# 64-column attention tiles, 64 queries of each image to a maxima tile, transposed reciprocals, and a GpSimd that waits for VectorE's sums

## What is computed

```python
Q = jnp.einsum('kc,bcp->bkp', q_w, xf)   # 16 x 3136
K = jnp.einsum('kc,bcp->bkp', k_w, xf)
V = jnp.einsum('vc,bcp->bvp', v_w, xf)   # 64 x 3136
S = jnp.einsum('bkp,bkq->bpq', Q, K)
A = jax.nn.softmax(S, axis=-1)
z = jnp.einsum('bpq,bvq->bvp', A, V)
```

## Time and profile before

| what | value |
|---|---|
| median of 3 runs | 2080.59 us (2080.13 to 2082.37) |
| the profiled execution's own time | 2084.49 us |
| its span, from first to last instruction | 2082.7 us |
| mean granted TensorE clock, of 2.4 GHz | 0.924 |
| busy share of the span: PE, DVE, ACT, POOL | 90%, 77%, 42%, 64% |

### The profile page before, as it was taken

One profiled execution on the slowest core, in us unless ns is written; L12 is line 12 of the kernel. 1 busy time (PEld: TensorE's weight loads), 2 busy tenths in 40 slices (PEclk: granted clock), 3 DMA queues, 4 the chain that ended last, 5 costly groups with the idle time before them and its releaser, 6 DMA issues.

```text
span 2082.7 us, 30055 instructions
## 1 busy us (share of the span) xinstructions
PE 1869.7 (90%) x7932; PEld 696.8 (33%) x7932; DVE 1596.4 (77%) x2642; ACT 865.8 (42%) x1064; POOL 1341.5 (64%) x702
## 2 busy tenths in 40 slices
PE   5877999999878799999987789999998779999996
PEld 4352222223336122222333622222233442222221
DVE  5747888887874788888786478888879557888883
ACT  2132554546314145454622324545461333454553
POOL 3510788989650179898954037989886205798887
PEclk9986999999888699999988869999999887999998
DMA  1003000000000300000000210000000030000000
GB/s 76 0 0 78 1 6 5 5 8 7 6 1 12 66 1 6 10 5 4 5 6 1 37 41 6 5 5 5 4 5 5 0 47 0 6 5 5 4 4 9
DMA packets 8505, 26.08 MB, mean 13 GB/s; under 512 B 2256, under 2 KB 5840, under 8 KB 7888
## 3 DMA queue, kind: packets, MB, share of 16 engines
q1 hardware_dynamic: 8400, 24.79, 5.1%
HBM read 8.73 MB, written 6.42 MB: 7 GB/s over the span
## 4 chain that ended last, share of the span: by engine, by line
PE 63%; issue 13%; DVE 10%; POOL 9%; ACT 2%; SPq 1%; DMA 1%; POOLq 1%; DVEq 0%; ACTq 0%
PE PS L1165 27%; PE PS L1112 14%; PE PS L1097 11%; DVE nmt L617 3%; DVE nmt L610 2%; POOL accP L943 2%; DVE accD L694 2%; POOL VT L905 1%; PE PS L1083 1%; POOL VT L900 1%; POOL VT L902 1%; PE PS L1070 1%; PE PS L1061 1%; POOL VT L909 1%; PE PS L1122 1%
## 5 line engine op out<-in xcount | busy, mean ns | idle before, releaser
L826 ACT ACTIVATE Pb<-PS 128x896 f32<-128x896 f32 (+1 forms) x700 | 640.5, 917 | 629.2 <-PE PS L1112 611.4
L943 POOL TENSOR_TENSOR accP<-accP,Pb 128x896 f32<-128x896 f32 x364 | 832.3, 2287 | 46.3 <-ACT Pb L826 20.5
L610 DVE TENSOR_REDUCE nmt<-PS 128x1 f32<-128x448 f32 x1176 | 663.6, 613 | 164.1 <-PE PS L1097 163.2
L1165 PE MATMUL PS<-Pb,VT 128*64 128x448 f32 x2800 | 693.5, 573 | 11.9 <-ACT Pb L826 9.3
L1112 PE MATMUL PS<-Qa,Ka 99*128 (+3 forms) x1400 | 478.3, 363 | 1.0 <-ACT Qa L810 1.0
L1097 PE MATMUL PS<-Ka,Qa 96*128 96x448 bf16 x1176 | 394.4, 356 | 24.3 <-DVE nmt L610 23.4
L694 DVE TENSOR_TENSOR accD<-accD,Pb 128x896 f32<-128x896 f32 x168 | 301.8, 1796 | 42.2 <-ACT Pb L826 40.6
L1112 PEld LDWEIGHTS PS<-Qa,Ka 99*128 99x128 bf16 (+1 forms) x1400 | 125.1, 98 | 540.5 <-issue 490.2
L936 POOL TENSOR_TENSOR accQ<-Pb 128x896 f32<-128x896 f32 x28 | 61.7, 2203 | 267.2 <-ACT Pb L826 267.2
L1165 PEld LDWEIGHTS PS<-Pb,VT 128*64 128x64 f32 x2800 | 145.7, 136 | 239.0 <-issue 193.5
L526 DVE SCALAR_TENSOR_TENSOR Pb<-PS,cf,xnp 128x448 f32<-128x448 f32 x252 | 154.8, 675 | 12.6 <-PE PS L1020 8.8
(11 more groups left out here) (138 smaller groups left out, 1488.4 us busy)
## 6 DMA issues: line engine op xcount, KB each, us to landing
xin<-in_x SPq DMA_DIRECT2D x4, 1568.0 KB, 6.6
out<-xw SPq DMA_DIRECT2D x28, 224.0 KB, 1.9
Qa<-parts SPq DMA_DIRECT2D x48, 98.0 KB, 4.0
Ka<-parts SPq DMA_DIRECT2D x48, 98.0 KB, 4.1
wz<-in_weights SPq DMA_DIRECT2D x1, 829.0 KB, 7.9
cs<-in_cst SPq DMA_DIRECT2D x1, 576.0 KB, 8.5
wz<-in_weights SPq DMA_DIRECT2D x1, 576.0 KB, 9.4
cs<-in_cst SPq DMA_DIRECT2D x1, 256.0 KB, 6.3
```

The costliest lines, as they stand in the source:

```text
L610: nc.vector.reduce_max(nmt[:, i // NJ, i % NJ:i % NJ + 1], PS[0:BLK, bank, 0:CH], X, negate=True).then_inc(mx_free, 1)
L826: nc.scalar.activation(Pb[0:r, j % PSLOTS, :, :], PS[0:r, b:b + 2, 0:CH], ACT.Exp).then_inc(exp_done, 1)
L943: nc.gpsimd.tensor_tensor((accQ if j < TO_ACCP else accP)[:, :, :], (accQ if j <= TO_ACCP else accP)[:, :, :], Pb[:, j % PSLOTS, :, :], AL ...
L1165: last = mm(PS[C * h:C * h + C, OB, 0:CH], VT[:, j, C * h:C * h + C], Pb[:, j % PSLOTS, h, :], start=(j == 0), stop=(j == NQ - 1))
```

## The change

- Maxima tiles: a tile is now 64 queries of each of the two images by 448 keys, made by two matmuls of 64 columns that write the lower and the upper 64 partitions of one bank (`tile_of`). A superblock has 7 x 7 = 49 tiles; 49 instead of 56 come before the first step. PSUM rows, maxima and split are laid out accordingly.
- Scores: 128 keys are made by two matmuls of 64 columns instead of one of 128.
- SP issues the spreading DMAs by part, both halves of a part together, and TensorE waits for both halves before the first tile.
- Reciprocals: one 32 x 32 block transpose of the denominators (each is equal over 64 partitions), a reciprocal of 14 columns, and a transpose back with the 14 columns broadcast, all three in step 3, instead of four reciprocals of 112 columns in steps 3 to 6.
- GpSimd waits for VectorE's sum of step j-1 before its own sum of step j (at steps 4, 8, 12, 16, 20), and at step 1 for all sums of the superblock before.
- The superblocks of a group are written out one by one on TensorE and VectorE.

```diff
-TILES = 2 * NJ
-PAIR_TILES = 7 * TILES
-FIRST_TILES = 4 * TILES
+TILES = NJ * NJ
+GROUP_TILES = (NJ - 1) * TILES
...
-                for h in range(2):
-                    for part, ready in enumerate((part_h, part_m, part_l)):
-                        if h == 0:
-                            sp.wait_ge(ready, NJ * g + NJ)
+                for part, ready in enumerate((part_h, part_m, part_l)):
+                    sp.wait_ge(ready, NJ * g + NJ)
+                    for h in range(2):
                         spread(part, h)
...
-                def reciprocals(sidx, i):
-
-                    if i == 0:
-                        dve.wait_ge(d_ready, sidx + 2)
-                        dve.wait_ge(fin_done, sidx + 1)
-                    ins = nc.vector.reciprocal(Rr[:, i * QUART:(i + 1) * QUART], PS[:, 7, i * QUART:(i + 1) * QUART])
-                    if i == 3:
-                        ins.then_inc(recip, 1)
+                def reciprocals(sidx):
+
+                    dve.wait_ge(d_ready, sidx + 2)
+                    dve.wait_ge(fin_done, sidx + 1)
+                    nc.vector.transpose(Rr[:, :], PS[:, 7, 0:CH]).then_inc(rstep, 1)
+                    dve.wait_ge(rstep, 2 * sidx + 1)
+                    nc.vector.reciprocal(Rc[:, :], Rr[:, 0:CH:SQ]).then_inc(rstep, 1)
+                    dve.wait_ge(rstep, 2 * sidx + 2)
+                    nc.vector.transpose(Rr[:, :].rearrange("p (a b) -> p a b", b=SQ),
+                                        Rc[:, :].unsqueeze(2).to_broadcast([P, CH // SQ, SQ])).then_inc(recip, 1)
...
                             pool.wait_ge(exp_done, NQ * sidx + j + 1)
                             if j == 1:
+                                pool.wait_ge(psum_dve, NDVE * (sidx + 1))
+                            if j - 1 in DVE_SUMS:
+                                pool.wait_ge(psum_dve, NDVE * (sidx + 1) + dve_sums_upto(j - 1))
+                            if j == 1:
...
+                def tile_of(bank, s, i):
+
+                    blk, t = i // NJ, i % NJ
+                    for h in range(2):
+                        last = mm(PS[C * h:C * h + C, bank, 0:CH], Qa[0:KROWS, h, s * CH + blk * C:s * CH + blk * C + C],
+                                  Ka[0:KROWS, h, t * CH:(t + 1) * CH], start=True, stop=True)
+                    return last
...
                     j = k % NQ
-                    r = key_rows(j)
-                    ins = mm(PS[0:r, 2 * (k % 2) + h, 0:CH], Ka[0:KROWS + 3, h, j * QC:j * QC + r],
-                             Qa[0:KROWS + 3, h, ds(s * CH, CH)], start=True, stop=True)
+                    for c in range(0, key_rows(j), C):
+                        ins = mm(PS[c:c + C, 2 * (k % 2) + h, 0:CH], Ka[0:KROWS + 3, h, j * QC + c:j * QC + c + C],
+                                 Qa[0:KROWS + 3, h, s * CH:(s + 1) * CH], start=True, stop=True)
...
-                for i in range(FIRST_TILES):
-                    h, blk, t = i // (FIRST_TILES // 2), i // NJ % 4, i % NJ
-                    if i % (FIRST_TILES // 2) == 0:
-                        pe.wait_ge(qk_loaded[h], 16 * (SPREADS * (g + 1) + 1))
+                for loaded in qk_loaded:
+                    pe.wait_ge(loaded, 16 * (SPREADS * (g + 1) + 1))
+                for i in range(TILES):
```

More of the change, by code:

```diff
@@ L43 @@
 KROWS = 6 * DK
-QUART = CH // 4
+SQ = 32
 BLK = 128
@@ L78, in plan_tiles @@
 def plan_tiles():
-    plan, steps, held = [], [], {4: 0, 5: 0, 7: 0}
-    early = 3 * TILES
-    for span, tiles in ((range(0, SPLIT_STEP + 1), early),
-                        (range(SPLIT_STEP + 1, NQ + SPLIT_STEP + 1), PAIR_TILES - early)):
-        total = sum(DENSITY[i % NQ] for i in span)
-        done = 0
-        for i in span:
-            steps += [i] * (round(tiles * (done + DENSITY[i % NQ]) / total) - round(tiles * done / total))
-            done += DENSITY[i % NQ]
-    for i, step in enumerate(steps):
-        banks = (4, 5, 7) if step % NQ in FREE7 else (4, 5)
-        bank = min(banks, key=lambda b: held[b])
-        plan.append((step, bank, held[bank]))
-        held[bank] = i + 1
+    plan, held = [], {4: 0, 5: 0, 7: 0}
+    for s in range(1, NJ):
+        end = NQ * (s - 1) + SPLIT_STEP + 1
+        span = range(0 if s == 1 else end - NQ, end)
+        total = sum(DENSITY[k % NQ] for k in span)
+        done = 0
+        for k in span:
+            upto = done + DENSITY[k % NQ]
+            for _ in range(round(TILES * upto / total) - round(TILES * done / total)):
+                bank = min((4, 5, 7) if k % NQ in FREE7 else (4, 5), key=lambda b: held[b])
+                plan.append((k, bank, held[bank]))
+                held[bank] = len(plan)
+            done = upto
     return plan
@@ L695, in superblock @@
                                                         ALU.add).then_inc(psum_dve, 1)
[L697 removed]
+                for i in range(TILES):
                     first_tile(i)
[L699 to L712 removed]
+                dve.wait_ge(first_used, TILES * (g + 1) + NJ)
+                split_max(NJ * g)
+                for s in range(NJ):
+                    superblock(s)
+                reciprocals(NJ * g + NJ - 1)
             front_stats(0)
@@ L827, in exps @@
                                              ACT.Exp).then_inc(exp_done, 1)
-                        if j == ROWS_STEP + 2 and rows_of:
-                            max_rows(sidx + 1, *rows_of)
+                        if j == ROWS_STEP + 2 and rows_of is not None:
+                            max_rows(sidx + 1, rows_of)
                         if front_of is not None:
@@ L1141, in front_at, with superblock @@
                             front_transpose(g + 1, i)
-                def superblock(s, half, base, col, first):
+                def superblock(s):
                     sidx = NJ * g + s
@@ L1149, in superblock @@
                     for j in range(NQ):
-                        k = NQ * (half % 2) + j
-                        tiles = [] if half == 2 else [i for i in tiles_at(k) if not first or i >= EARLY_TILES]
+                        k = NQ * s + j
+                        tiles = [i for i in tiles_at(k) if i >= EARLY_TILES]
                         def next_tile(seen7):
@@ L1203, in group @@
                         scores(j, 0, h)
-                pair_of(0, True)
-                with pe.Fori(1, NJ // 2) as t:
-                    pair_of(t, False)
-                superblock(NJ - 1, 2, 0, 0, False)
+                for s in range(NJ):
+                    superblock(s)
                 denominators(NJ * g + NJ - 1)
```

124 lines of the change are left out of this document (50 added, 74 removed).

## The result

The changed kernel takes 2124.4 us (median of 4 runs, 2120.6 to 2131.9) against 2081.5 for the kernel before beside it: 1.0208 of its time, 95% interval 1.0192 to 1.0224, 43 us slower. The forecast was 2101, 21 us slower: the sign was right, the size half. The profiled span is 2124.3 us, 41.6 more than before.

What follows compares the result with a forecast made beforehand. TensorE was taken to set the pace, GpSimd and VectorE close behind, its saving lost to GpSimd's longer round. Terms 4.8 + 2.2 + 1.9 - 4.0 + 0.4 = 5.3 us a group, 21 in four: 2101 us, range 2035 to 2125.

Steps and rivals of the forecast that it cites:

- TensorE's part: TensorE's work in a superblock: a step of 1.53 instead of 1.78 us, about 40.5 us in all, some 7 less.
- GpSimd's part, superblocks 1 to 4: Walk from denominators to denominators: 48.4 us a round, 193.6 for four against 191.4 before, +2.2 us a group.
- Theory A: Follow-up experiments' theory: a superblock's round is closed by GpSimd's wait for step 3's copy, 4.1 us behind the denominators.
- the wait of step 4: GpSimd's sum of step 4 waits for VectorE's copy, starting 4.05 us after the denominators; TensorE's saved 7 us become waiting.
- Superblock 0: First superblock of a group: no denominators before it, GpSimd's new wait short, -4.0 us a group off 57.2.
- Superblock 6: Last superblock of a group: +2.3 us for GpSimd's steps 4 and 20, -1.9 for shorter reciprocals, +0.4 a group.
- Superblock 5: Superblock without tiles in its last steps: 47.3 us instead of 45.4, +1.9 us a group.
- the held banks: At a superblock's end, reductions behind VectorE's late sum hold TensorE's two banks; worth 1.2 us a round.
- Before the first step: Start of a group: first tile 8.5 us later, waiting for all 24 DMAs; fewer reductions -3.7; +4.8 us a group.
- The faster one: Rival: GpSimd's waits find VectorE done, the round falls towards GpSimd's floor; 2023 us, halfway 2060 likelier; chance 0.30.
- The slower one: Rival: VectorE's load makes TensorE wait for banks and GpSimd run dry, 1 to 2 us a superblock; 2125 to 2145; chance 0.10.
- Pairs that do not overlap: Rival: 64-column matmul pairs run one after the other (2330 us), or weight loads come out (2175); chance 0.03.

Runs made afterwards that it cites:

- a9: Changed kernel with GpSimd's sums of the exponentials over only the first 224 of 448 queries: 1937.5 us, ratio 0.9310 to the kernel before.
- a7: Changed kernel with VectorE's copy of step 3 placed ahead of the transposes and short reciprocal: 2091.1 us, ratio 1.0047 to the kernel before.
- a3: Changed kernel with the four reciprocals of 112 columns at steps 3 to 6 put back: 2106.9 us, ratio 1.0114 to the kernel before.
- b1: Kernel before with GpSimd's six waits a superblock as the only change: 2103.8 us, ratio 1.0105.
- a1: Changed kernel without any of GpSimd's six waits a superblock for VectorE's sums: 2105.4 us, ratio 1.0121 to the kernel before.
- a2: Changed kernel without GpSimd's wait of step 4 alone, the other waits kept: 2100.0 us, ratio 1.0090 to the kernel before.
- a4: Changed kernel without GpSimd's waits and with the four short reciprocals put back: 2079.2 us, ratio 0.9982 to the kernel before.
- b2: Kernel before with the transposed reciprocals as the only change: 2113.2 us, ratio 1.0155.
- a10: Changed kernel with VectorE's tile reductions, once the steps have begun, over 224 of 448 keys: 2099.1 us, ratio 1.0109 to the kernel before.
- a14: Changed kernel, copy of step 3 ahead of the transposes, GpSimd waiting only at 1, 12, 16, 20 (mostly only 1 in superblock 6): 2064.3 us, ratio 0.9910.
- a15: Changed kernel, copy of step 3 ahead of the transposes, GpSimd waiting only at step 1: 2062.5 us, ratio 0.9913 to the kernel before.

## Why the prediction was right about the sign and wrong about the size

Of the 20 us between forecast and measurement, superblock 0 makes 8, superblock 5 makes 7, superblock 6 makes 6 and superblock 1 makes 2, less 3 at the start of the groups. The steps that failed are the prediction's terms for superblocks 0, 6 and 5: it let GpSimd's new waits cost next to nothing there. The paragraphs below take them in turn, after the parts that held.

**TensorE's part: right in kind, too large.** The pairs overlap, the loads hide, the changes of form are gone. The step was read as 1.53 us and is 1.52. The superblock was put at 40.5 us, where TensorE needs up to 42.7 (a9, busy 97%); the saving is 4.9 us, not 7. What fills the 2 us between was not followed. As the saving is all lost to GpSimd this moved the forecast by nothing.

**GpSimd's part, superblocks 1 to 4: right by its walk.** From the denominators to GpSimd's sum of step 4: 4.14 us measured (4.05 forecast), from there to the end of step 22's sum 38.9 (39.1), to the next denominators 5.36 (5.3). The round of 48.4 came out to the tenth in superblocks 2 to 4; superblock 1 took 49.0, 2 us over the four groups. The terms of its 39.1 add up to 39.3 as they stand there. Theory A's forecasts for a7, a3 and b1, made from the same chain, held too; those for a1 and a2 did not.

**But the chain was taken for the whole reason.** The prediction gave the growth of the round to the wait of step 4. a1, a3, a4, b1 and b2 show that the change has two causes of like size, either of which alone is enough to take back what TensorE saves (us):

| | without waits | with waits |
|---|---|---|
| before | 2081 | 2104 |
| before, transposes | 2113 | not run |
| 64 columns and tiles | 2079 | 2107 |
| the same, transposes | 2105 | 2124 |

The transposes cost 18 to 31 us, the waits 19 to 28, and the two together 45. The third row is a4: its 2 us are some 20 gained in the superblocks, less what the later first tiles cost. In the prediction the transposes stand only as durations ahead of GpSimd's wait. Beside the waits that is what they cost (a3: 0.8 us a round for as much of VectorE's time ahead of the copy, 1.5 instead of 0.8). Without the waits, where it had no price for them, the copy behind them is caught by GpSimd's sum, and they cost 1.6 us a round in b2.

**Superblock 0: the step that failed first.** "GpSimd's new wait is short there". The timeline of GpSimd in superblock 0:

```profile
212.87 2.08 POOL L932 TENSOR_TENSOR accQ<-accQ,Pb 128x896 f32<-128x896 f32 x1 [0.66 <-ACT Pb L811]
218.92 2.09 POOL L932 TENSOR_TENSOR accQ<-accQ,Pb 128x896 f32<-128x896 f32 x1 [3.98 <-DVE accD L684]
```

VectorE ahead of its copy there:

```profile
216.72 1.16 DVE L608 TENSOR_REDUCE nmt<-PS 128x1 f32<-128x448 f32 x2 [0.36 <-PE PS L1087]
217.79 0.62 DVE L684 COPY accD<-Pb 128x896 f32<-128x896 f32 x1
```

It waits 3.98 us, nearly as long as elsewhere. There are no denominators, but VectorE's copy stands behind reductions of tiles that TensorE delivers two a step. Superblock 0 gains 1.9 us, not 4.0: 8 us of the error. Without that wait (a2) it is some 1.4 us shorter in three of the groups, with halved reductions (a10) 2.0 to 3.0; the wait and VectorE's load both have a part, and how they share it stays open.

**Superblock 6: the second.** "GpSimd's step 4 moves behind the denominators and its step 20 behind VectorE's late sum, +2.3, and three quarters of reciprocals less at the end ... give 1.9 back". GpSimd there:

```profile
508.81 2.08 POOL L932 TENSOR_TENSOR accQ<-accQ,Pb 128x896 f32<-128x896 f32 x1 [2.65 <-DVE accD L684]
...
533.85 6.41 POOL L932 TENSOR_TENSOR accP<-accP,Pb 128x896 f32<-128x896 f32 x3 [1.11 <-DVE accD L688]
546.51 2.08 POOL L932 TENSOR_TENSOR accP<-accP,Pb 128x896 f32<-128x896 f32 x1 [6.26 <-ACT Pb L811]
```

For step 20 the row names an exponential, but that of step 20 ended at 537.60; what came last was VectorE's sum of step 19, which stands behind the next group's front work:

```profile
545.26 1.09 DVE L688 TENSOR_TENSOR accD<-accD,Pb 128x896 f32<-128x896 f32 x1
```

GpSimd waits at steps 4, 16 and 20 (2.65, 1.11 and 6.26 us), and the superblock is 1.3 to 2.9 us longer than before. b1 shows 1.6 us from the waits alone; a1, without them, is still 0.7 to 0.9 longer, for a reason that stays open. At the end the shorter reciprocals gave back 1.4 us once, in the last group: in the other groups nothing waits for them. 6 us of the error.

**Superblock 5: the third.** "By the same walk without the held banks it comes to 47.3". It is 48.1 and 48.3 in groups one and four, as GpSimd's sums from step 4 on take 40.2 instead of 39.1 us: VectorE's sums of steps 11 and 15 make it wait 1.1 us each, where they stretch one of its sums by 0.7 in the steady rounds, and its last two sums take 2.81 us each instead of one. That these waits are the cause a1 shows: without any, superblock 5 takes 45.2 us in all four groups. In groups two and three it is 49.3 and 50.3. Windows (columns as above) of the seam in groups two and three:

```profile
1017.00:1022.00 5.00, 2.70 (x16) 0.94 (x16) 4.94 (x7) 2.20 (x3) 4.84 (x3) 1.00 0.00 0
1022.00:1026.00 4.00, 3.07 (x14) 1.07 (x16) 1.21 (x4) 1.80 (x3) 3.92 (x3) 0.77 0.00 0
...
1540.00:1546.00 6.00, 4.06 (x24) 1.39 (x24) 5.96 (x6) 2.27 (x3) 5.84 (x3) 1.00 0.00 0
1546.00:1549.50 3.50, 2.42 (x10) 1.01 (x12) 2.16 (x6) 1.73 (x2) 3.42 (x3) 0.55 0.00 0
1549.50:1552.00 2.50, 2.50 (x10) 0.75 (x7) 0.00 (x0) 0.92 (x1) 0.77 (x1) 0.50 0.00 0
```

TensorE, without tiles there and waiting for the exponentials, is busy 54% in one and 68% in the other stretch, and then the granted clock is 0.77 in group two, 0.55 and 0.50 in group three, that is at last wholly the lower level of 1.2 GHz. From the first of the denominators of group three to TensorE's next instruction pass 3.2 us instead of 1.7. In group one TensorE was as little busy (49% from 499 to 504) and the clock stayed at 1.00; why the groups differ stays open. Before, with TensorE 96% busy in that place, the clock stayed at 1.00. The idle time that the change gives TensorE is paid for again there. 7 us of the error, some 3 of them by the clock, an estimate from what groups two and three take over group one (1.2 and 2.2 us).

**Before the first step: right, and 3 us too large.** The tile was forecast 8.5 us later and came 7.0 later, as SP's 24 DMAs begin 1.15 us sooner and take 16.0 us instead of 16.6; the reductions -3.7 as forecast. 4.8 us a group were forecast and 3.1 to 4.9 came.

**The rivals.** The faster one rested on a floor of 42.5 to 44.5 us for GpSimd's round. The chain in the trace, with no wait for the copy, makes 44.2 (48.4 less 4.16), and a14 and a15, nearest to it, reach 45.8 and 46.2 us, both at about 2063 us. The slower one, VectorE's load, does not hold for the steady rounds, which a10 shortens by 0.8 us; in superblock 0 it has a part. Pairs that do not overlap: refuted by the timeline.
